# A two-layer decoder on one core: transposes and routing of the experts moved into layer 1's last phase, a mask table fetched in layer 0

## The reference

```python
x = _layernorm(x + _L0_attn_ref(x, Wq, Wk, Wv, Wo))          # layer 0: linear attention, 16 heads
x = _layernorm(x + _L0_xattn_ref(x, ctx, ctx, ...))          # gated recurrence in matrix form
x = _layernorm(x + _L0_ffn_ref(x, w1, w3, w2, wr))           # feed forward, top 2 of 8 rows
x = _layernorm(x + _L1_attn_ref(x, Wq, Wk, Wv, Wo, rms_w))   # layer 1: decayed attention
x = _layernorm(x + _L1_xattn_ref(x, ctx, ctx, gamma))        # softmax over 512 features, 8 heads
x = _layernorm(x + _L1_ffn_ref(x, Wg, W1, W3, W2, Ws1, Ws3, Ws2))  # 16 experts, top 4, and a shared one
```

## Time and profile before

| | |
|---|---|
| median of 3 runs | 2804.14 us (2802.6 to 2809.92) |
| profiled execution, its own time | 2810.36 us |
| its span, first to last instruction | 2808.3 us |
| mean granted clock of TensorE | 0.971 |
| layer 0 | 0 to about 1101 us |
| layer 1 | 1101.8 to 1863 us |
| experts | 1864.0 us to the end |

### The profile page before, as it was taken

One profiled execution on the slowest core, in us unless ns is written; L12 is line 12 of the kernel. 1 busy time (PEld: TensorE's weight loads), 2 busy tenths in 40 slices (PEclk: granted clock), 3 DMA queues, 4 the chain that ended last, 5 costly groups with the idle time before them and its releaser, 6 DMA issues. The chain is left out here.

```text
span 2808.3 us, 33548 instructions
## 1 busy us (share of the span) xinstructions
PE 2625.8 (94%) x10885; PEld 1331.6 (47%) x10945; DVE 1390.3 (50%) x2555; ACT 840.2 (30%) x1899; POOL 527.8 (19%) x564
## 2 busy tenths in 40 slices
PE   8999999999999966899999999769999999999998
PEld 4544554555455443334344344124466556556543
DVE  4555664564657262577777777616322222222256
ACT  2324332442353231145555555530011111111101
POOL 2111101110211001322233233000011111111054
PEclk9999999999999987899999999989999999999999
DMA  6120122122202302335444544430123333332155
GB/s 198 60 75 30 50 86 90 61 76 77 73 31 75 117 1 86 76 71 115 102 104 112 107 100 110 113 144 0 47 99 127 127 131 129 127 129 98 53 146 157
DMA packets 108715, 260.60 MB, mean 93 GB/s; under 512 B 19554, under 2 KB 53218, under 8 KB 97074
## 3 DMA queue, kind: packets, MB, share of 16 engines
q1 hardware_dynamic: 95890, 220.42, 26.5%
q0 software_dynamic: 11440, 37.50, 4.5%
q10 hardware_dynamic: 1264, 1.10, 0.1%
HBM read 203.45 MB, written 55.13 MB: 92 GB/s over the span
## 5 line engine op out<-in xcount | busy, mean ns | idle before, releaser
L2569 PE MATMUL d_bank<-d_w,d_xcol 128*128 x1264 | 401.6, 461 | 0.0
L2103 DVE TENSOR_REDUCE c_mx<-c_pair 128x2 f32<-128x1024 f32 x256 | 303.8, 1217 | 110.1 <-PE c_pair L1976 109.2
L1853 ACT ACTIVATE c_probs<-c_exp 128x512 f32<-128x512 f32 x512 | 277.9, 597 | 218.5 <-PE c_exp L1990 165.0
L2569 PEld LDWEIGHTS d_bank<-d_w,d_xcol 128*128 128x128 f32 x1264 | 228.8, 191 | 101.5 <-issue 1.7
L642 POOL TENSOR_TENSOR a_ry<-h_ahead,a_rt 128x512 f32<-128x512 f32 x80 | 130.4, 1630 | 750.0 <-DVE a_rt L1175 750.0
L904 PE MATMUL a_bank<-h_quarters,a_ring 128*128 128x512 f32 x608 | 270.1, 595 | 0.0
L904 PE MATMUL a_bank<-h_ahead,h_rows 128*128 128x512 f32 x512 | 222.4, 592 | 0.0
L2576 PE MATMUL d_bank<-h_ahead,d_hid 128*128 x480 | 219.1, 592 | 0.7 <-DVE d_hid L2807 0.7
L226 PE MATMUL c_step<-h_quarters,h_ahead 128*128 128x512 f32 x360 | 173.2, 604 | 4.0 <-DVE h_ahead L265 2.2
L904 PEld LDWEIGHTS a_bank<-h_quarters,a_ring 128*128 128x128 f32 x608 | 113.5, 191 | 130.7 <-issue 127.8
L1990 PE MATMUL c_exp<-c_qs,c_ks 128*128 128x512 bf16 x453 | 147.8, 386 | 24.2 <-ACT c_probs L1853 9.2
(11 more groups left out here) (313 smaller groups left out, 3596.5 us busy)
## 6 DMA issues: line engine op xcount, KB each, us to landing
d_w<-in_w SPq DMA_DIRECT2D x16, 1408.0 KB
scratch_results<-d_yrow SPq DMA_DIRECT2D x80, 256.0 KB
a_ring<-in_wq SPq DMA_DIRECT2D x16, 1024.0 KB, 4.8
h_ahead<-in_wo SPq DMA_DIRECT2D x16, 1024.0 KB, 4.9
c_ks<-scratch_kpark SPq DMA_DIRECT2D x96, 128.0 KB, 4.5
c_qs<-scratch_qpark SPq DMA_DIRECT2D x96, 128.0 KB, 4.3
h_ahead<-in_w SPq DMA_DIRECT2D x16, 768.0 KB
a_ring<-in_w SPq DMA_DIRECT2D x8, 1024.0 KB, 7.9
```

Source lines behind the costliest of these rows:

```text
L1853: act.activation(probs[:, (LC * CH * n + k) % RING, :], bank[:, :], ACT.Exp, scale=float(CD) ** -0.5).then_inc(exped.sem, 1)
L2103: dve.tensor_reduce(mx[:, n % 2, at0:at0 + 2], bank[:, :].rearrange("p (i n) -> p i n", i=2), AX.X, ALU.max).then_inc(maxed.sem, 1)
L2569: ins = pe.matmul(bank[:, 0:FI], xcol[:, v, k, :], w13[:, bass.ds(at, 1), which, k, :].rearrange("p a n -> p (a n)"), start=(k == 0), stop ...
```

## The change

1. The transposes of the fifteen sequences 4 to 15 and 1 to 3 and the routing of groups 1 to 3 stand at the end of layer 1's list on PE. ACT's copies stand in phase 16, slot 1, behind the copy of the last sums and ahead of the root of the last norm. They use the halves of the two pair banks. In the experts' block only sequence 0 and group 0 are left, then the logits' transposes. The routing weights are fetched in phase 14.
2. In the experts' block SyncE loads ws1 and ws3 (1408 KB each) first, then five small tables, then ws2 (1536 KB), then the first expert (1408 and 768 KB). PE waits for ws1, ws3 and the tables ahead of the first shared product and for ws2 ahead of the first down product; DVE waits for the tables at its head, as before.
3. The mask table, the RMS weights and gamma are loaded by `Home.fetch` in layer 0, behind layer 1's weights.
4. DVE's fill of `ks` stands behind the first mask. SyncE ends layer 0 behind the issue of its last two stores; SyncE and POOL wait for them at the start of layer 1.
5. Memory is laid out anew for this: `stacks`, `xT`, the logits, layer 0's rows and work areas share one buffer, `ahead` grows from 10 to 14 rows of 512.

```diff
@@ class Home
+    LATE_IN = FIRST_IN + 16 * 3
+    AHEAD = [*range(GB, SEQS), *range(1, GB)]
...
+        self.stacks = sb("stacks", [P, 3 * SEQS * 2 * P])
+        self.xT = self.stacks[:, 0:SEQS * D].rearrange("p (c n) -> p c n", c=KC)
...
+        self.ahead = sb("ahead", [P, 14 * D])
+        self.decay = self.ahead[:, 10 * D:14 * D].rearrange("p (r c n) -> p r c n", r=HR, c=KC)
...
+        for dst, src in ((self.decay, "decay1"), (self.rms, "rms1"), (self.gamma, "gamma1")):
+            sp.dma_start(dst[:], t[src]).then_inc(chunk_in[2], 16)
+
+    def turn_row(self, pe, bank, b):
+        for c in range(KC):
+            ins = pe.transpose(bank[:, c * P:(c + 1) * P], self.y[:, b, c * P:(c + 1) * P], self.ident[:, :])
+        return ins
+
+    def route(self, pe, bank, g):
+        for c in range(KC):
+            ins = pe.matmul(bank[0:NE, :], self.wg[:, c, :], self.xT[:, c, GT * g:GT * (g + 1)],
+                            start=(c == 0), stop=(c == KC - 1))
+        return ins
+
+    def turned_row(self, act, bank, b):
+        act.activation(self.xT[:, :, b * P:(b + 1) * P], bank[:, :].rearrange("p (c n) -> p c n", c=KC),
+                       ACT.Copy).then_inc(self.xT_ready, 1)
+
+    def routed(self, act, bank, g):
+        act.activation(self.logits[:, g, :], bank[0:NE, :], ACT.Copy).then_inc(self.xT_ready, 1)
@@ build_layer0, sync
-            sp.dma_start(t["fsum"], fsum[:, :]).then_inc(fstored.sem, 16)
-            sp.wait_ge(fstored.sem, 16)
-            stored.wait(sp, GROUPS, 0)
+            sp.dma_start(t["fsum"], fsum[:, :]).then_inc(home.fstored, 16)
+            stored.wait(sp, GROUPS - 1, 0)
@@ build_layer1
+        seam_order = [("xt", b) for b in Home.AHEAD] + [("rl", g) for g in range(1, GROUPS)]
+        seam = Tiles([two[:, 512 * i:512 * i + 512] for two in pair_banks for i in range(2)],
+                     ctx.enter_context(nc.semaphore("c_filled_seam")), seam_order,
+                     lambda key: (Signal(home.xT_ready), seam_order.index(key) + 1))
@@ build_layer1, sync (gpsimd has the same two waits at its head)
+            home.stored.wait(sp, GROUPS, 0)
+            sp.wait_ge(home.fstored, 16)
             for n in range(2):
                 load_c(n)
                 load_cT(n)
-            for dst, src in ((decay, "decay1"), (rmsw, "rms1"), (gamma, "gamma1")):
-                sp.dma_start(dst[:], t[src]).then_inc(late.sem, 16)
...
                     rows_of_experts(3)
+                    sp.dma_start(home.wg[:], t["wg1"]).then_inc(chunk_in[3], 16)
@@ build_layer1, scalar
+                    if done == SEQS - 1 and i == 1:
+                        for kind, n in seam_order:
+                            bank = seam.wait(act, 0, (kind, n))
+                            if kind == "xt":
+                                home.turned_row(act, bank, n)
+                            else:
+                                home.routed(act, bank, n)
@@ build_layer1, tensor
+            for b in Home.AHEAD:
+                if b % GB == 0 or b == 1:
+                    pe.wait_ge(chunk_in[b // GB], home.y_in(b))
+                bank = seam.start(pe, 0, ("xt", b), [(exped, LC * CH * SEQS)])
+                seam.done(home.turn_row(pe, bank, b))
+            for g in range(1, GROUPS):
+                bank = seam.start(pe, 0, ("rl", g), [(Signal(home.xT_ready), len(Home.AHEAD))])
+                seam.done(home.route(pe, bank, g))
@@ build_layer1, vector
-            dve.memset(ks[TR:, :, :, :].rearrange("p s h n -> p (s h n)").bitcast(F32), two_ones)\
-               .then_inc(stacks_set.sem, 1)
             dve.wait_ge(consts.sem, NC)
...
                     if a1 is not None and i == SCORES + 1:
                         mask(a1)
+                    if a1 == 0 and i == SCORES + 1:
+                        dve.memset(ks[TR:, :, :, :].rearrange("p s h n -> p (s h n)").bitcast(F32), two_ones)\
+                           .then_inc(stacks_set.sem, 1)
@@ build_experts, sync
-            for dst, src in ((wg, "wg1"), (iota, "iota1"), (causal, "causal"), (steps_of, "steps_of"),
+            for dst, src in ((ws1, "ws1"), (ws3, "ws3")):
+                sp.dma_start(dst[:], t[src]).then_inc(shared_in.sem, 16)
+            for dst, src in ((iota, "iota1"), (causal, "causal"), (steps_of, "steps_of"),
                              (block_no, "block_no"), (spots, "spots")):
                 sp.dma_start(dst[:], t[src]).then_inc(weights.sem, 16)
-            for dst, src in ((ws1, "ws1"), (ws3, "ws3"), (ws2, "ws2")):
-                sp.dma_start(dst[:], t[src]).then_inc(shared_in.sem, 16)
+            sp.dma_start(ws2, t["ws2"]).then_inc(shared_in.sem, 16)
@@ build_experts, tensor
-            for b in TURNED:
...
-            pe.wait_ge(weights.sem, 16 * 6)
-            for n, g in enumerate(ROUTED):
...
+            pe.wait_ge(chunk_in[0], home.y_in(0))
+            bank = first.start(pe, 0, ("xt", 0))
+            first.done(home.turn_row(pe, bank, 0))
+            bank = first.start(pe, 0, ("rl", 0), [(xT_ready, SEQS + GROUPS - 1)])
+            first.done(home.route(pe, bank, 0))
...
-            pe.wait_ge(shared_in.sem, 48)
+            pe.wait_ge(shared_in.sem, 32)
             pe.wait_ge(consts.sem, CONSTS)
+            pe.wait_ge(weights.sem, 16 * 5)
```

More of the change, by code:

```diff
@@ L1784, in _ @@
         def _(pool):
+            home.stored.wait(pool, GROUPS, 0)
+            pool.wait_ge(home.fstored, 16)
             pool.memset(ones[:], 1.0).then_inc(consts.sem, 1)
@@ L2051, in _ @@
                         steps.done(ins)
+            for key in pair_order[-2:]:
+                sig, count = drained(key)
+                sig.wait(pe, 0, count)
+            for b in Home.AHEAD:
[6 more added lines that the diff above has]
+                seam.done(home.route(pe, bank, g))
         @block.vector
         def _(dve):
-            two_ones = 1.0019378662109375
-            dve.memset(ks[TR:, :, :, :].rearrange("p s h n -> p (s h n)").bitcast(F32), two_ones)\
-               .then_inc(stacks_set.sem, 1)
             dve.wait_ge(consts.sem, NC)
@@ L2216, in build_experts @@
         xrow = home.ahead[:, 2 * NI * D + 2 * GT:2 * NI * D + 2 * GT + 2 * D].rearrange("p (u d) -> p u d", u=2)
[L2217 removed]
+        xcol = home.ahead[:, 10 * D:12 * D].rearrange("p (u c n) -> p u c n", u=2, c=KC)
         gate = sb("gate", [P, 2, FI])
[L2219 to L2220 removed]
+        at0 = SEQS * D + 4 * D
+        hrow, hid = (home.stacks[:, at0 + 2 * FP * n:at0 + 2 * FP * (n + 1)].rearrange("p (u f) -> p u f", u=2)
+                     for n in range(2))
+        yrow = home.ahead[:, 12 * D:14 * D].rearrange("p (u d) -> p u d", u=2)
         SLOTS = 4
[L2222 to L2223 removed]
+        back = home.stacks[:, SEQS * D:SEQS * D + SLOTS * D].rearrange("p (s d) -> p s d", d=D)
+        logits_of = home.logits
         iota, ident, causal, ones = sb("iota", [P, NE]), home.ident, sb("causal", [P, P]), sb("ones", [P, P])
@@ L2426, in _ @@
             act.wait_ge(consts.sem, CONSTS)
-            for b in TURNED:
-                bank = first.wait(act, 0, ("xt", b))
-                act.activation(xT[:, :, b * P:(b + 1) * P], bank[:, :].rearrange("p (c n) -> p c n", c=KC),
-                               ACT.Copy).then_inc(xT_ready.sem, 1)
-            for g in ROUTED:
-                bank = first.wait(act, 0, ("rl", g))
-                act.activation(logits_of[:, g, :], bank[0:NE, :], ACT.Copy).then_inc(xT_ready.sem, 1)
+            home.turned_row(act, first.wait(act, 0, ("xt", 0)), 0)
+            home.routed(act, first.wait(act, 0, ("rl", 0)), 0)
             act.wait_ge(rt_shift.sem, 1)
```

79 lines of the change are left out of this document (32 added, 47 removed).

## The result

| | before | after |
|---|---|---|
| median, of 4 runs each | 2805.4 us (2802.6 to 2809.9) | 2786.2 us (2785.2 to 2786.8) |
| profiled execution, its own time | 2810.36 us | 2785.16 us |
| its span | 2808.3 us | 2783.2 us |
| mean granted clock of TensorE | 0.971 | 0.978 |

The ratio is 0.9929, with an interval of 0.9916 to 0.9942: 20 us less, 16 to 24. The forecast was 17.7 us less. Another execution of the same kernel, `again`, gives 0.9932. The profiled execution of before is at the high end of its runs, so the spans differ by 25.1 us, more than the kernels do.

What follows compares the result with a forecast made beforehand. TensorE, busy 94% of the span, was taken as the bound, with time to win only where it idles between stages. Gains of 11.7 and 6.0 us sum to 17.7, so 2804.1 becomes 2786.4 us, range 2779 to 2799.

Steps and rivals of the forecast that it cites:

- The seam: Layer 1 to experts: transposes and routing moved into TensorE's idle time start the shared products 11.7 us sooner, 9 to 14.
- root held: End of layer 1: ScalarE's routed copies delay the last norm's root, moving the tail and the experts' start by 1.3 us.
- landing of sequence 0: Start of the experts' block: sequence 0's rows land 2.8 us after their load is issued.
- group 0, partly at the lower clock: Experts' block: eight routing matmuls, 3.5 us at full clock or 6.9 at the lower; the middle, 5.2, was taken.
- The start of layer 1: Layer 0 to layer 1: earlier table loads bring masks 9.1 us and scaling 6.7 us sooner; 6.0 gained, bounds 4 and 9.
- the pause's clock: Start of layer 1: a longer pause lowers TensorE's clock for the first output product's eight matmuls; 0.7 us taken off.
- Rival 1: Experts' block: a load sets the shared products' start; 4 us gained there, 10 in all, 2794 us; chance 0.08.
- Rival 2: End of layer 1: transposes do not keep the clock, root 9.5 us late; 9.5 us gained, 2794.6 us; chance 0.09.
- rival 4: End of layer 1: TensorE stays at the lower clock, root 17 us late; slower, 2806.6 us; chance 0.03.
- Rival 3: Start of layer 1 gives its gain back, a transfer or buffer holding the second or third sequence; 2792.4 us; chance 0.08.

Runs made afterwards that it cites:

- warm: Kernel after plus 16 routing matmuls whose products nothing reads, filling TensorE's pause before the last sequence; 2790.7 us, 0.995 of before.
- undo_masks: Kernel after with only the mask table's loads and the place of the key stack's fill put back; 2791.62 us, 0.9948 of before.
- undo_both: Kernel after with both moves put back, keeping memory layout, load order, earlier end of layer 0 and routing-weights fetch; 2801.49 us, 0.999 of before.
- fill_behind: Kernel after with VectorE's fill of `ks` moved behind the first scaling; 2784.06 us, 0.9931 of before.
- warm_start: `fill_behind` plus six unread matmuls behind the first scores at the start of layer 1; 2783.09 us, 0.9927 of before.
- combined: `fill_behind`, `warm_start` and `warm` in one, plus the last norm's root ahead of ScalarE's last routed copy; 2777.38 us, 0.9911 of before.
- warm_tables: `warm` with the five small tables fetched in phase 14 of layer 1 instead of the experts' block; 2785.98 us, 0.9919 of before.
- combined_tables: `combined` with the five small tables fetched in phase 14 of layer 1; 2780.86 us, 0.9903 of before.

## Why the prediction was right

The time, 2786.2, is the forecast to 0.2 us; that closeness is luck, since the interval of the gain is 16 to 24 us. The mechanism and its two terms are what the runs bear out: 11.8 and 5.0 us, each within some 4 to 5, with 0 to 5.6 for everything else, against 11.7, 6.0 and 0.

**The seam**, step by step, measured from the end of the last attention product:

| step | forecast | measured |
|---|---|---|
| transposes, paced by ScalarE's copies | 7.5 | 7.45 |
| routing of three groups, 24 matmuls | 10.4 | 10.47 |
| end of the seam | 19.35 | 19.23 |
| root held | 1.3 | 1.03 |
| experts' block starts | 23.25 | 23.0 |
| landing of sequence 0 | 2.8 | 3.8 |
| group 0, partly at the lower clock | 5.2 | 5.55 |
| shared products start | 35.25 | 35.3 |

The landing took 1.0 us more. The two shared tables are now issued 0.73 us behind it (at 1855.07), but with the same order it took 2.6 us in `warm`, 3.1 in `undo_masks` and 3.6 in `again`, so what made up the 1.0 us is not shown. GpSimd's fills, which the forecast had as the last thing ahead of ScalarE's copy, were over at 1858.78 (1858.04 + 0.74), and the copy came at 1859.40, behind the transposes: 27.33 behind the product's end, where the forecast's 1869.0 is 26.95. The forecast had TensorE and the loads ready at the same moment, about 1877. In the kernel after the loads had 1.1 us to spare, and `warm` shows that they become the gate once TensorE's chain is shorter by 2 us.

**The start of layer 1** is the step that was mis-sized. Masks were forecast 9.1 us sooner and came 8.9 sooner. The scaling was forecast 6.7 us sooner and came 5.2 sooner. The working had the fill at 5.18 us directly behind the masks; what it lacked is the 1.34 us that the fill waits before it starts. The row of before carried a bracket for this fill too, "5.65 <-issue", at the head of the list. The other engines' first instructions of the block start at 1101.79 to 1102.09, and the fill at 1103.12, 1.33 us behind the first of them: the trace of before had it. For the pause's clock I took 0.7 off; the first output product took 6.42 instead of 5.59, 0.83. To the end of that product 4.4 us are gained instead of 6.0, and the halves undone give 5.0. C, which goes on to the first copy of attention sums, is 5.8 us shorter than before in `after` and 6.4 in `again`, so some of it seems to come back. Where is not shown; one place where the two differ is the granted clock from 1155 to 1160. Of before and of after:

```profile
1155.00:1160.00 5.00, 5.00 (x12) 2.59 (x13) 3.09 (x3) 0.46 (x2) 0.00 (x0) 0.50 0.33 37
```

```profile
1155.00:1160.00 5.00, 4.80 (x15) 1.83 (x14) 4.43 (x8) 0.50 (x2) 0.00 (x0) 1.00 0.00 0
```

**Rival 1** (the tables' landing) was false as a loss and true as a place: its price is zero in the kernel after and 2.07 us in `warm`. I had priced it with all loads mixed, everything in at 1885, 19.7 us behind the block's start; in `warm` the small tables were in 12.5 us behind it.

**Rival 2 and rival 4** (a lower clock in the seam) are false: 60 transposes took 6.96 us on TensorE, 0.116 each, at a granted clock of 1.00. By the Trainium skill, "TensorE: Matmul & The Clock Gate", Part 4, the clock would not engage for them; for this form of transpose the trace of after disagrees, as that of before did.

**Rival 3** (the gain of the start given back) is false: from one first copy of attention sums to the next, the first twelve phases of before and of after take 42.45 us each, but for one of before that took 43.29, and the lead that after has at the first copy is still there at the fourteenth. The last two phases vary by 1 to 2.5 us among kernels of either kind (D is 619.6 in `undo_both`, 621.2 in `again`).

**What two spans alone would say.** From the two profiled executions alone the change gains 25.1 us. By the table that is 11.6 in E, 5.8 in C, 3.4 in D, 3.6 in F and 0.9 in layer 0. D, F and layer 0 vary by as much between kernels that do not differ there: F is 915.8 in `after` and 922.6 in `again`.

## What to carry to other kernels

Where one stage hands over to the next through HBM, look for work of the next stage whose inputs are long there, put it into the pause, and price it twice: what it removes behind the seam, and how long it holds the engine that the last small chain needs. Before making such a seam faster still, list all that lands near its end: here three gates stood within 2 us, and keeping the clock up in the pause moved nothing by itself. Split the gain by distances inside a profile and by kernels with one half undone, as two whole spans can differ by 10 us with the same instructions.

## What the runs showed of the hardware that was not expected

- The fill of 32 partitions by 6144 elements on VectorE begins 1.33 or 1.34 us behind whatever stands ahead of it: the masks (after), the scaling (`fill_behind`, `warm_start`), GpSimd's last fill that it waits for (1104.12 to 1105.45 in `undo_masks`), the block's start (before). It then takes 5.18. GpSimd's fill of the same size takes 5.22 and has no such gap (1104.17 in `undo_masks`). What the 1.34 us are was not tried.
- TensorE's clock fell from 1.00 to 0.50, that is from 2.4 to 1.2 GHz, within a pause of 7.5 us, and read 1.00 again from 1865 on, where work had begun at 1858.19. Sixteen unread matmuls in that pause, and group 0's routing took 3.61 us instead of 5.55; behind a further pause of 2.07 us in `warm` and one of 0.76 in `combined` it read 0.50 again, and the next 48 products took 22.36 and 22.54 us, where they took 20.87 behind a pause of 0.57 in `warm_tables` and behind none in `combined_tables`.
- Gathers of result rows at the end of the experts took 3.3 to 3.7 us each on the chain of `again`; in `after` none was on the chain of the last 94 us.
